# A decoder layer on one core: order of the pieces in the passage between attention and the later layers

## The reference

```
x = x + attn(layernorm(x))      # per token: 16 heads of 16; products over the heads of ONE token
x = x + cross(layernorm(x), ctx)  # softmax over the 256 context rows of a unit
x = x + ffn(layernorm(x))       # two of 8 low-rank adapters per token, 1024 hidden, relu
```

## Time and profile before

| | us |
|---|---|
| median of 3 runs (697.99 to 701.59) | 700.67 |
| the profiled execution: its own time | 697.59 |
| its span, first to last instruction | 695.9 |
| granted TensorE clock, mean over the span | 0.956 of full |

### The profile page before, as it was taken

How to read it: one execution, slowest core, us unless ns; L and a number is a source line. 1 busy time by engine, 2 the same in 40 slices (tenths; PEclk the granted TensorE clock), 3 DMA queues, 4 the chain that set the end, 5 groups by cost and what they waited for, 6 DMA issues and landing times.

```text
span 695.9 us, 21635 instructions
## 1 busy us (share of the span) xinstructions
PE 634.3 (91%) x8338; PEld 596.2 (86%) x8338; DVE 504.7 (73%) x1242; ACT 367.8 (53%) x825; POOL 261.6 (38%) x361
## 2 busy tenths in 40 slices
PE   4799799799878886977999999999999999999997
PEld 3677687687667776867999999999999999999997
DVE  5686379497637797856787877787778877886672
ACT  3654366576464665743565455545554555455432
POOL 1212122221121634313454545454555455544322
PEclk9999899899798998997999999999999999999999
DMA  8686647575864466520001100110011011100000
GB/s 265 131 111 97 100 82 127 73 110 119 120 115 126 146 195 153 191 70 24 24 1 39 39 17 25 38 38 9 29 38 38 0 38 38 38 0 16 16 16 32
DMA packets 84140, 50.13 MB, mean 72 GB/s; under 512 B 31320, under 2 KB 83808, under 8 KB 84064
## 3 DMA queue, kind: packets, MB, share of 16 engines
q1 hardware_dynamic: 84064, 49.07, 32.0%
HBM read 23.88 MB, written 12.58 MB: 52 GB/s over the span
## 4 chain that ended last, share of the span: by engine, by line
PE 76%; DVE 10%; issue 6%; DMA 3%; ACT 2%; SPq 1%; POOL 1%; POOLq 0%; DVEq 0%; ACTq 0%
PE banks L711 59%; PE banks L837 5%; PE banks L766 3%; PE banks L855 3%; PE banks L996 2%; PE banks L873 2%; DMA m_w<-attn_scratch 1%; POOL f_hT_lo L2186 1%; DVE m_hT_lo L1693 1%; PE banks L780 1%; DVE h_sm L1682 1%; DVE m_y L1700 1%; DMA n_v<-in_L_attn_Wv_dram 1%; PE banks L735 1%; DMA x_scratch<-m_y 1%
## 5 line engine op out<-in xcount | busy, mean ns | idle before, releaser
L2186 POOL TENSOR_TENSOR f_hT_lo<-f_hs,f_hT_hi 128x512 fp32r<-128x512 f32 x64 | 87.3, 1365 | 102.8 <-ACT f_hT_hi L1401 99.2
L1877 DVE SCALAR_TENSOR_TENSOR f_hs<-banks,nbic,f_h 128x256 f32<-128x256 f32 x128 | 54.6, 478 | 40.9 <-PE banks L711 40.9
L711 PE MATMUL banks<-woT_hi,f_hT_lo 128*128 128x256 f32 x256 | 74.8, 292 | 0.2 <-POOL f_hT_lo L2186 0.2
L711 PE MATMUL banks<-f_adT_hi,lbT_lo 128*128 128x256 f32 x256 | 73.6, 287 | 0.0
L711 PE MATMUL banks<-f_xT_hi,wiT_hi 128*128 128x256 f32 x256 | 72.8, 284 | 0.0
L711 PE MATMUL banks<-f_xT_hi,wiT_lo 128*128 128x256 f32 x256 | 72.7, 284 | 0.0
L711 PE MATMUL banks<-woT_hi,f_hT_hi 128*128 128x256 f32 x256 | 72.5, 283 | 0.0
L711 PE MATMUL banks<-f_xT_lo,wiT_hi 128*128 128x256 f32 x256 | 72.5, 283 | 0.0
L711 PE MATMUL banks<-woT_lo,f_hT_hi 128*128 128x256 f32 x256 | 72.4, 283 | 0.0
L711 PE MATMUL banks<-f_adT_hi,lbT_hi 128*128 128x256 f32 x256 | 72.2, 282 | 0.0
L711 PE MATMUL banks<-f_adT_lo,lbT_hi 128*128 128x256 f32 x256 | 72.2, 282 | 0.0
(11 more groups left out here) (265 smaller groups left out, 1989.8 us busy)
## 6 DMA issues: line engine op xcount, KB each, us to landing
h_qk<-p_qk SPq DMA_DIRECT2D x64, 128.0 KB, 5.0
xin<-in_x_dram SPq DMA_DIRECT2D x16, 256.0 KB, 5.6
h_v<-p_v SPq DMA_DIRECT2D x128, 32.0 KB
attn_scratch<-h_wn SPq DMA_DIRECT2D x16, 256.0 KB, 3.6
m_x<-in_x_dram SPq DMA_DIRECT2D x16, 256.0 KB, 3.2
m_w<-attn_scratch SPq DMA_DIRECT2D x16, 256.0 KB, 3.4
x_scratch<-m_y SPq DMA_DIRECT2D x16, 256.0 KB, 3.3
c_x<-x_scratch SPq DMA_DIRECT2D x16, 256.0 KB, 2.8
```

The lines of the kernel that those rows point to most:

```text
L711: ins = pe.matmul(acc, left(a), right(b), start=first and n == 0, stop=last and n == 2, skip_group_check=skip)
L1877: ins = dve.scalar_tensor_tensor(out=f_hs[:, j % 2, c * T:(c + 1) * T], in0=bank[HB[j]][:, c * T:(c + 1) * T], scalar=nbic[:, f:f + 1], in ...
L2186: pool.tensor_tensor(lo, f_hs[:, j % 2], hi.bitcast(F32), ALU.subtract).then_inc(f_hlo, 1)
```

## The change

Nothing is added or taken away; pieces change place in the hand-written lists of the passage, and the head's root is cut into a first part (`head_guess`: scaling, guess and the first Newton round, five steps) and a second (`head_root`: the other two rounds, six steps), so that another piece can stand between.

```diff
 SP
             go(1, load_w, load_mx)
+            go(2, load_w)
+            go(3, load_w)
             go(7, tiles_in(0, 0), tiles_in(0, 1), tiles_in(0, 2), tiles_in(0, 3))
             go(3, store_w(0), store_w(1))
             go(7, values_in(0, 0), tiles_in(1, 0), tiles_in(1, 1), tiles_in(1, 2), tiles_in(1, 3))
-            go(2, load_w)
-            go(3, load_w)
 TensorE
-            go(7, turn_attn)
+            go(7, turn_attn, head_turn(2), head_turn(3))
             go(6, hidden)
             go(5, mixed)
-            go(7, head_turn(2), head_turn(3))
 ScalarE
-            go(7, head_natural(0), head_natural(1), m_split)
+            go(7, head_natural(0), head_natural(1), m_split, head_natural(2), head_natural(3))
             go(6, m_gelus)
-            go(7, head_natural(2), head_natural(3), head_squares)
+            go(7, head_squares)
             go(8, m_split)
+            go(7, m_gelus)
             go(6, head_squares3)
-            go(7, m_gelus)
             go(9, m_split)
-            go(6, head_third)
             go(8, m_gelus)
             go(0, c_split)
-            go(1, c_normalise)
+            go(6, head_third)
             go(10, m_split)
-            go(7, head_squares3)
             go(9, m_gelus)
             go(11, m_split)
-            go(7, head_third)
+            go(7, head_squares3)
             go(10, m_gelus)
             go(0, c_queries)
+            go(7, head_third)
             go(12, m_split)
             go(11, m_gelus)
+            go(1, c_normalise)
 VectorE
             go(2, m_residual)
-            go(1, c_moments)
             go(7, head_masked(1, 0), head_masked(1, 1))
             go(5, m_low)
             go(4, m_gsplit)
+            go(1, c_moments)
             go(6, head_sums)
+            go(3, m_residual)
             go(5, head_added)
-            go(3, m_residual)
-            go(6, head_newton, m_low, head_normal)
+            go(6, head_guess, m_low, head_root)
+            go(5, m_gsplit)
             go(4, m_residual)
-            go(5, m_gsplit)
             go(7, m_low)
+            go(6, head_normal)
+            go(6, m_gsplit)
+            go(5, m_residual)
             go(6, head_gain)
-            go(5, m_residual)
-            go(6, m_gsplit)
+            go(8, m_low)
             go(0, c_clow, c_constant)
+            go(7, m_gsplit)
+            go(6, m_residual)
             go(7, head_sums)
-            go(8, m_low)
-            go(6, m_residual)
-            go(7, head_newton, m_gsplit, head_normal)
             go(9, m_low)
+            go(7, head_guess)
+            go(8, m_gsplit)
             go(7, m_residual)
             go(6, head_added)
-            go(7, head_gain)
-            go(8, m_gsplit)
             go(10, m_low)
             go(0, c_low)
+            go(7, head_root)
+            go(9, m_gsplit)
+            go(7, head_normal)
             go(8, m_residual)
-            go(9, m_gsplit)
+            go(7, head_gain)
             go(11, m_low)
-            go(7, head_added)
-            spread_bias()
+            go(10, m_gsplit)
             go(9, m_residual)
-            go(10, m_gsplit)
             go(0, c_usplit)
             go(12, m_low)
+            go(7, head_added)
             go(10, m_residual)
...
-            go(15, m_gsplit, m_residual)
+            go(15, m_gsplit)
+            spread_bias()
+            go(15, m_residual)
 GpSimd
             go(0, c_constant, c_with_bias)
+            go(0, c_natural)
             go(1, c_rstds)
-            go(0, c_natural)
             go(6, m_with_x)
...
             go(10, m_with_x)
+            go(7, head_rthird)
             go(1, c_constant, c_with_bias)
-            go(7, head_rthird)
             go(11, m_with_x)
```

More of the change, by code:

```diff
@@ L1908, in head_sums, with root_step, newton, head_guess @@
                                   AX_X, ALU.add).then_inc(h_ssd, 1)
[L1910 to L1914, removed]
+            def root_step(u, ins, k):
+                ins.then_inc(h_rhd, 1)
+                dve.wait_ge(h_rhd, nth(u, ROOTS, k))
+            def newton(u, n):
+                root_step(u, dve.scalar_tensor_tensor(out=h_ss[:, :], in0=h_rh[:, :], scalar=-0.5, in1=h_ms[:, :],
+                                                      op0=ALU.mult, op1=ALU.mult), 3 * n + 3)
+                root_step(u, dve.tensor_tensor(h_ss[:, :], h_ss[:, :], h_rh[:, :], ALU.mult), 3 * n + 4)
+                root_step(u, dve.scalar_tensor_tensor(out=h_rh[:, :], in0=h_ss[:, :], scalar=1.5, in1=h_rh[:, :],
+                                                      op0=ALU.add, op1=ALU.mult), 3 * n + 5)
+            def head_guess(u):
                 dve.wait_ge(h_ssd, nth(u, 1, 1))
@@ L1918, in head_newton, with head_root @@
                     dve.wait_ge(h_n1d, nth(u, 1, 0))
[L1919 to L1926, removed]
+                root_step(u, dve.tensor_scalar(h_ms[:, :], h_ss[:, :], 1.0 / HD, RMS_EPS, ALU.mult, ALU.add), 1)
+                root_step(u, dve.tensor_scalar(h_rh[:, :].bitcast(I32), h_ms[:, :].bitcast(I32), -0.5, FIRST_ROOT,
+                                               ALU.mult, ALU.add), 2)
+                newton(u, 0)
+            def head_root(u):
+                for n in range(1, NEWTON):
+                    newton(u, n)
+            def head_newton(u):
+                head_guess(u)
+                head_root(u)
             def head_normal(u):
```

## The result

| | us |
|---|---|
| changed, median of 15 runs (703.41 to 712.16) | 705.61 |
| before, on the same chip, 15 runs (695.35 to 703.19) | 699.69 |
| ratio, 95% interval | 1.0094 [1.0073, 1.0115] |
| profiled execution of the changed kernel, own time / span | 703.53 / 701.8 |

The change costs 6.6 us by the ratio, which is formed of fast executions alone (one of the second measurement, at 1374.57 us, is not in it). That second measurement of the same code, experiment b4, gave 1.0067 [1.0032, 1.0102], 4.7 us. The forecast was 700.5, no change. Both measurements are slower than before; the first median lies outside the stated range of 695.7 to 704.8, the second (702.68) inside it.

A forecast was written before the change was run, and what follows sets the result against it. TensorE, waiting in order for loads and VectorE, was taken to bound the passage. 0 - 4.0 - 3.0 - 2.4 + 8.8 + 0.5 + 0.1 = 0.0 us, taken from the median of 700.67, gave 700.5; 80% range 695.7 to 704.8.

The forecast's parts named there:

- T3: Start of unit 3's turn on TensorE; predicted at 213.1 us where it was 217.17.
- T12: Start of unit 12's turn on TensorE; predicted at 269.3 us where it was 278.64.
- T13: Start of unit 13's turn on TensorE; predicted at 283.5 us where it was 284.07.
- Part 1: Loads of units 2 and 3 issued earlier on SP: T3 4.0 us earlier, lower bound 1.9.
- Part 2: VectorE's c_moments(1) behind the masks: last head values start 7.0 us earlier in all, 3.0 of it new.
- Part 3: Head root in halves on VectorE, mixing ahead of heads: 2.4 us of the 9.4 us gain at T12.
- Part 4: Late c_normalise(1) delays GpSimd's m_with_x(11), then SP's load_mx(13) and load_w(13), so T13: 8.8 us lost.
- slower rival: Queue behind load_mx(13): gain(7) ends after 270, T13 at 287.5, 704.5 us in all; chance 0.22.
- Part 5: Behind T13: TensorE begins at 1.2 GHz, sum +0.5 us; spread_bias on VectorE adds +0.1.
- faster rival: Same mechanism, but loads land near 3.1 us and T12 is at 266.4: 697.5 to 695 us; chance 0.27.
- the change does not act at the front: hidden(1) gains but the scores don't, 1.9 us in place of 4.0: 702.6 us; chance 0.06.

The follow-up runs named there:

- a1: Changed kernel with m_with_x(11) and m_with_x(12) ahead of c_constant(1) and c_with_bias(1) on GpSimd; 697.56 us, 0.9982 of before.
- b2: b1 with load_w(13), and also store_x1(9), ahead of the store of super-unit 7's first half on SP; 692.33 us, 0.9907 of before.
- a4: Kernel before with only c_moments(1) moved behind the last masks and m_gsplit(4) on VectorE; 699.84 us, 1.0010 of before.
- c2: b2 with VectorE's list put back to that of the kernel before, except the moments, kept behind the masks; 700.54 us, 1.0019 of before.
- d1: Changed kernel with load_mx(13) behind the store of super-unit 7's first half and load_w(13) on SP; 698.71 us, 0.9975 of before.
- a2: Kernel before with c_normalise(1) behind m_gelus(11) on ScalarE and head_rthird(7) ahead of c_constant(1) on GpSimd; 706.61 us, 1.0130 of before.
- b1: a1 with super-unit 7's last two head quarters put back behind mixed(5) on TensorE and m_gelus(6) on ScalarE; 696.00 us, 0.9952 of before.

## Why the prediction was wrong

The mechanisms were there, one by one; the sum of +0.0 was not. The profiled executions differ in H by 3.56, so the predicted marks, which are in before's own time, are compared after taking that off.

| mark | predicted | measured, less 3.56 |
|---|---|---|
| T3 | 213.1 | 214.9 |
| last values | 231.8 | 233.5 |
| T7 | 242.0 | 243.3 |
| T8 | 247.2 | 249.4 |
| gain(7) ends | 266.6 | 268.1 |
| T12 | 269.3 | 270.1 |
| T13 | 283.5 | 285.9 |

- **Part 1, -4.0, was -2.3.** T2 is 4.3 us earlier as said and the early loads wait for nobody, but the argument that behind the scores "nothing but TensorE and the mask counts" left out the gap in the scores, 3.03 us for 1.38 (the whole of the missing 1.7), which ends behind a transfer of instructions. In the repeat of the changed kernel, where it was 1.45, T3 is 3.1 earlier. The lower bound of 1.9 holds in these two; a1 and b2, with the same early loads, have 1.85 and 1.88.
- **Part 2, -3.0 at the last values, was -3.0**: 5.26 in all, 2.29 of it T3's. Taken alone (a4) its time can't be told from nothing; that it needs part 3 behind it is likely and wasn't tried.
- **Part 3, -2.4, was -3.2**: T12 came 8.5 earlier (9.2 in the repeat) for 9.4, and 2.3 and 3.0 of that are parts 1 and 2. Lags of 1.3 and 2.2 behind the forecast at T7 and T8 had shrunk to 0.8 by then. c2 puts the new order at 5.0 us at T12, with ScalarE's list unfit for the old one. The wait for quarter 0's store was named; it decides nothing.
- **Part 4, +8.8, was +10.3 and +10.0.** The queue is the one described: a1 and d1 cut it on two engines and get the same 8 us back from the first measurement (6 from the second), a2 makes it alone. From the end of gain(7) to T13 it took 17.75 us against 16.9 written down: 6.86 to c_normalise (7.0 predicted), then GpSimd 4.4 for 4.0, where c_with_bias took 1.92 in place of 1.43, then issue and landing 5.4 for 4.8. The 1.43 is the first tail unit's row; the second one's, in the same trace of before, is 1.88 at 270.73, and that was the piece to price. The rest is that T12 ran 0.7 us less behind gain(7) than forecast: part of the front's gain can't reach T13, as the slower rival said.
- **Part 5, +0.6, was +1.7 (+0.7 in the repeat).** The clock's price was read from one gap of 3.00 us; behind 10.58 us all 4.56 us that follow ran at 1.2 GHz, 22 matmuls for the twelve allowed for. It isn't the length of the stand: b1 pays as much behind 4.15 us, and the repeat, behind 10.74, was at 0.50 for 2.24 us and at 0.71 over the next 2.30.

**The step that failed is the sum of parts 4 and 5**: 9.4 was written where the two profiles have 12.0 and 10.6, and the gains ahead of T12 of 9.4 were 8.5 and 9.2. So the passage became 3.5 us longer (1.4 in the repeat), not 0.0. Inside part 4 the stretch up to c_normalise was right within 0.2 us; what was short were GpSimd's pieces and the landing, priced at a row taken undisturbed and at one load's 3.70.

The "slower" rival, 704.5, came nearest in time. Its mechanism is what part 4 is, but its trigger, gain(7) after 270 in before's time, was not met (268.1), and T13 is at 285.9, not at the 287.5 it gave. That its time came out is in part luck: the passage is 3.5 us longer, the rest of the timed loss isn't explained. The faster rival, loads near 3.1 us, fell: T12 was never at 266.4. That the change does not act at the front fell too.

**What stays open.** Timed, the loss is 4.7 to 6.6 us; the profiled passages account for 1.4 to 3.5. From the mean passage of the two profiles of before, the three with the 10 us stand (changed, its repeat, a2) are timed 3.4 to 3.8 us longer than their passages say; the nine other experiments lie between -2.2 and +2.4 around theirs, 0.3 on average. H doesn't explain it: its mean is 197.4 over the nine profiles with early loads and 197.2 over the five with late ones, and the loop behind takes the same time at a granted clock of 1.00. All three are seen in one profiled execution each, and the changed kernel's and a2's profiled executions are among the fastest of their runs (703.53 in 703.41 to 712.16; 704.97 is the lowest). What the other executions do more of was not seen.

## What to carry to other kernels

When a piece is moved on one engine, follow what is queued behind every piece that waits for it, on each in-order queue in turn, down to the DMA issues: c_normalise(1) was harmless late, but GpSimd's and SP's lists carried its lateness to a load that needs nothing of it, and moving two lines on GpSimd or one on SP gave 6 to 8 us back. Cut one such edge and look again, since a second can stand hidden behind it (here the store ahead of load_w(13), 0.45%). Price each piece of a serial chain from its own row, not from its twin's elsewhere (1.88 us here for 1.43), and the low clock behind a stand from several rows, since one row of 3.00 us idle gave +0.6 where five profiles paid 0.7 to 1.7. When a list is put back to test it, put back the lists that were written to fit it as well, or the misfit is measured too.

## What the runs showed of the hardware

- After 10.58 us of idle time TensorE ran at least 4.56 us at 1.2 GHz, 22 matmuls, though busy all the time, and after 4.15 us (b1) 4.39 us, 21 matmuls; after 1.14 us (b2) it ran at 2.4 GHz. After 3.87 us (d1) it began at a granted clock of 0.89 for 1.87 us and then ran 3.00 us at 0.50.
- GpSimd's c_with_bias (two instructions) took 1.43 us for the first tail unit of before, and 1.88 (before) and 1.92 (changed) for the second. A head product on VectorE took 1.22 us at 270.47, with GpSimd idle, and 2.32 us when GpSimd's m_with_x had begun 0.06 us ahead of it; these are the rows of VectorE and of GpSimd in the changed kernel:

```profile
253.90 2.32 DVE L1945 TENSOR_TENSOR h_wn<-h_wn,g2row 128x1024 f32<-128x1024 f32 x1
```
```profile
253.84 1.29 POOL L2146 TENSOR_TENSOR m_w<-m_w,m_x 128x512 f32<-128x512 f32 x1 [4.82 <-DMA m_x<-in_x_dram]
```

The second keeps its 1.29 us, and the first is longer by 1.10. The Trainium skill, "SBUF — State Buffer", section "Who interferes with whom", has a VectorE instruction with two SBUF inputs and a GpSimd instruction that reads SBUF exclude each other, with the earlier one undisturbed; the two rows agree.

- A run of 128 small matmuls stops 1.1 to 3.6 us two matmuls before its end, and longer in most kernels whose loads were issued early. It is not the only such gap: between 20 and 330 us the fourteen profiles have 108 gaps of TensorE of 1 us or more with "issue" for a releaser, and each ends 1.1 to 2.1 us (nine in ten: 1.3 to 1.8) after a 16 KB transfer of kind "instruction" on queue 8 has landed. No experiment was made on it.
- A store of h_wn, issued at 244.04, took 5.6 us until ScalarE could go on; the loads of m_w took 4.1 in the stretch before T13.
